# A six-stage decoder on one core: tokens quantized and the residual added by GpSimd in the feed-forward stage, tokens loaded first in three stages

## The reference, cut to what matters

```python
def _act_quant(x):
    scale = 127.0 / jnp.clip(jnp.max(jnp.abs(x), axis=-1, keepdims=True), 1e-05)
    xq = jnp.clip(jnp.round(x * scale), -128.0, 127.0) / scale
    return x + jax.lax.stop_gradient(xq - x)

def _bitlinear(x, w):
    return jnp.einsum('bsi,oi->bso', _act_quant(x), _weight_quant(w))
...
    return _bitlinear(gate * up, w_down)
```

## Time and profile before

| | |
|---|---|
| median of 3 runs | 3903.01 us (3902.52 to 3906.85) |
| profiled execution | 3898.5 us, its span 3896.7 us |
| busy over the span | PE 85%, DVE 81%, ACT 71%, POOL 67% |
| stages, from the timeline | first 0 to 333, cross-attention 337 to 842, expert 845 to 1229, Mamba 1232 to 3132, second cross-attention 3135 to 3568, feed-forward 3571 to the end |
| granted TensorE clock | 0.948 of full over the span |

### The profile page before, as it was taken

One profiled execution on the slowest core, in us unless ns is written; L12 is line 12 of the kernel. 1 busy time (PEld: TensorE's weight loads), 2 busy tenths in 40 slices (PEclk: granted clock), 3 DMA queues, 4 the chain that ended last, 5 costly groups with the idle time before them and its releaser, 6 DMA issues. The chain is left out here.

```text
span 3896.7 us, 75270 instructions
## 1 busy us (share of the span) xinstructions
PE 3307.6 (85%) x23328; PEld 2500.1 (64%) x23360; DVE 3169.0 (81%) x5291; ACT 2775.3 (71%) x5061; POOL 2609.6 (67%) x2794
## 2 busy tenths in 40 slices
PE   8996888879964688898898889888888869997887
PEld 5664666667542467676777767676766757775554
DVE  5665888855386799899899989989999759998888
ACT  2223777744475788888888888888888647777777
POOL 1222666630085699999899988989999836664555
PEclk9998999979976899999999999999999989999999
DMA  1111122242112111111111111111111112221111
GB/s 60 56 56 53 41 51 51 45 101 51 48 44 72 42 51 56 54 48 55 49 52 55 56 54 48 53 51 51 54 50 50 41 48 74 72 53 56 61 54 39
DMA packets 285487, 209.64 MB, mean 54 GB/s; under 512 B 131353, under 2 KB 249689, under 8 KB 285161
## 3 DMA queue, kind: packets, MB, share of 16 engines
q1 hardware_dynamic: 285160, 205.72, 19.0%
HBM read 149.18 MB, written 51.41 MB: 51 GB/s over the span
## 5 line engine op out<-in xcount | busy, mean ns | idle before, releaser
L2884 POOL TENSOR_TENSOR ma_ch<-ma_h,ma_crep 128x512 f32<-128x512 f32 x1024 | 1371.8, 1361 | 157.0 <-DVE ma_h L2986 142.8
L2986 DVE TENSOR_TENSOR_SCAN ma_h<-ma_a,ma_pbu 128x512 f32<-128x512 f32 x1024 | 1212.7, 1206 | 173.7 <-PE ma_pbu L2564 114.1
L2564 PE MATMUL ma_pbu<-ma_ident,ma_bu 128*128 128x128 f32 x4096 | 660.3, 285 | 198.9 <-DVE ma_h L2986 158.6
L2564 PEld LDWEIGHTS ma_pbu<-ma_ident,ma_bu 128*128 128x128 f32 x4096 | 480.3, 145 | 440.8 <-DVE ma_h L2986 312.6
L2771 ACT ACTIVATE ma_a<-ma_dt,ma_A 128x510 f32<-128x510 f32 x1024 | 653.3, 718 | 1.4 <-issue 1.4
L2573 PE MATMUL ma_py<-ma_ident,ma_ch 128*128 128x128 f32 x4096 | 626.2, 279 | 0.8 <-POOL ma_ch L2884 0.8
L2762 ACT ACTIVATE ma_bu<-ma_uT,ma_b_t 128x512 f32<-128x512 f32 x784 | 508.1, 718 | 17.1 <-PE ma_pbu L2564 15.4
L2573 PEld LDWEIGHTS ma_py<-ma_ident,ma_ch 128*128 128x128 f32 x4096 | 497.6, 145 | 1.2 <-POOL ma_ch L2884 1.2
L1571 POOL TENSOR_TENSOR xa_prob<-xa_e,xa_rec_head 128x616 f32<-128x616 f32 x128 | 155.7, 1218 | 126.0 <-DVE xa_rec_head L1663 113.9
L921 POOL TENSOR_TENSOR xa_prob<-xa_e,xa_rec_head 128x616 f32<-128x616 f32 x128 | 155.7, 1217 | 109.3 <-DVE xa_rec_head L1013 93.1
L359 POOL TENSOR_TENSOR la_veps<-la_mv,la_eps 128x2 f32<-128x2 f32 x32 | 6.3, 197 | 249.9 <-DVE la_mv L392 249.9
(11 more groups left out here) (372 smaller groups left out, 8007.0 us busy)
## 6 DMA issues: line engine op xcount, KB each, us to landing
ma_crep<-ma_ct_dram SPq DMA_DIRECT2D x256, 256.0 KB
xa_x<-act SPq DMA_DIRECT2D x64, 256.0 KB, 3.0
act<-xa_y SPq DMA_DIRECT2D x64, 256.0 KB, 3.1
la_x<-in_x SPq DMA_DIRECT2D x32, 256.0 KB, 2.6
act<-la_y SPq DMA_DIRECT2D x32, 256.0 KB, 2.2
ea_x<-act SPq DMA_DIRECT2D x32, 256.0 KB, 11.5
act<-ea_x SPq DMA_DIRECT2D x32, 256.0 KB, 4.0
ma_x<-act SPq DMA_DIRECT2D x16, 512.0 KB, 4.6
```

The source lines that it names most:

```text
L2564: last = pe.transpose(pbu[c % 2][:, t * P:(t + 1) * P], bu[:, s % 2, t, c * P:(c + 1) * P], ident[:, :])
L2884: pool.tensor_tensor(ch[:, s % 2, c], h[:, s % 2, c], crep[:, s % 4, :], ALU.mult).then_inc(multiplied, 1)
L2986: dve.tensor_tensor_scan(out=h[:, s % 2, c, :], data0=a[:, s % 2, c, :], data1=pbu[c % 2][:, :], initial=0.0, op0=ALU.mult, op1=ALU.add).t ...
```

## The change

In the feed-forward stage the quantization of the tokens (`scale_x`) goes from ScalarE to GpSimd, with a spacer before it, and waits there for the previous batch's transposes. ScalarE instead scales the down product out of PSUM into a new tile `scaled` (`scale_down`), GpSimd adds x to it (`residual`), and VectorE keeps the statistics alone (`moments`). In the first stage the identity and the tokens of batch 0 are loaded before the weights and turned before the wait for them. In both cross-attentions the token load goes out after the eighth of the 12 spreads. In the second one batch 0 is turned before the wait for the weights, and the bias work comes after its scores. In the expert stage the first group of tokens is loaded and waited for in two halves.

```diff
         block = st.block()
-        loads = ((ident[:, :], ident_d), (blocks[:, :], blocks_d),
+        loads = ((blocks[:, :], blocks_d),
                  (wq[:, :, :], wqT.rearrange("(c p) f -> p c f", p=P)),
...
         def _(sp):
+            sp.dma_start(ident[:, :], ident_d).then_inc(i_loaded, 16)
+            sp.dma_start(x[:, 0], batch_tiles(x_in, 0)).then_inc(x_loaded[0], 16)
             for dst, src in loads:
                 sp.dma_start(dst, src).then_inc(w_loaded, 16)
-            for b in range(PER):
+            for b in range(1, PER):
                 sp.dma_start(x[:, b], batch_tiles(x_in, b)).then_inc(x_loaded[b], 16)
...
+            pe.wait_ge(i_loaded, 16)
+            turn(0, 0)
             pe.wait_ge(w_loaded, 16 * len(loads))
-            turn(0, 0)
             in_turns(pe, batch, B // PER, PER, (0, 1, -1))
...
+            turned(0, 0)
             act.wait_ge(w_loaded, 16 * len(loads))
-            turned(0, 0)
             in_turns(act, batch, B // PER, PER, (0, 1, -1))
...
-            def spread_v(n):
+            def spread_v(n, meanwhile=None):
...
                     sp.wait_ge(oT_made, 2 * n - 2)
-                for lo, hi in pieces:
+                for i, (lo, hi) in enumerate(pieces):
+                    if meanwhile is not None and i == 8:
+                        sp.wait_ge(res_added, meanwhile)
+                        load_x((meanwhile + 3) % 4, meanwhile + 3)
                     h, k = lo // CTX, lo // P
...
                 if n + 1 < B:
-                    spread_v(n + 1)
-                if n >= 1 and n + 3 < B:
-                    sp.wait_ge(res_added, n)
-                    load_x((n + 3) % 4, n + 3)
+                    spread_v(n + 1, n if n >= 1 and n + 3 < B else None)
                 if n >= 3:
...
+            pe.wait_ge(setup_done, 1)
+            turn_x(0, 0, None)
+            turn_ctx(0, 0)
             pe.wait_ge(w_loaded, 16 * len(loads))
-            pe.wait_ge(setup_done, 1)
+            project_kv(0, 0)
+            project_q(0, 0, None)
+            scores(0, 0, 0)
             if bv_d is not None:
...
                 last.then_inc(bv_turned, 1)
+            turn_x(0, 1, None)
+            if bv_d is not None:
                 pe.wait_ge(bv_copied, 1)
...
                 pe.wait_ge(bo_ready, 1)
-            turn_x(0, 0, None)
-            turn_ctx(0, 0)
-            project_kv(0, 0)
-            project_q(0, 0, None)
-            scores(0, 0, 0)
-            turn_x(0, 1, None)
             batches(pe, batch)
...
                 norm_apply(0, 0)
+            copy_x(0, 0)
+            copy_ctx(0, 0)
             act.wait_ge(w_loaded, 16 * len(loads))
             if bq_d is not None:
-                act.wait_ge(bv_turned, 1)
-                act.activation(bvT[:, :, :].rearrange("p c q -> p (c q)"), pG[0][:, 0:D], ACT.Copy).then_inc(bv_copied, 1)
                 act.activation(bq4[:, :], bqk[:, 0, :], ACT.Copy, scale=0.25).then_inc(bq4_ready, 1)
                 act.wait_ge(bq4_ready, 1)
-            copy_x(0, 0)
-            copy_ctx(0, 0)
             if normed:
...
             copy_q(0, 0)
+            if bv_d is not None:
+                act.wait_ge(bv_turned, 1)
+                act.activation(bvT[:, :, :].rearrange("p c q -> p (c q)"), pG[0][:, 0:D], ACT.Copy).then_inc(bv_copied, 1)
             expo(0, 0, 0)
...
             dve.sem_inc(setup_done, 1)
-            if bv_d is not None:
-                dve.wait_ge(w_loaded, 16 * len(loads))
-                dve.wait_ge(bv_made, 1)
-                dve.tensor_tensor(bo[:, :], bo[:, :], pG[0][:, D:2 * D], ALU.add).then_inc(bo_ready, 1)
             if normed:
...
             unit(0, 0, 1)
+            if bv_d is not None:
+                dve.wait_ge(w_loaded, 16 * len(loads))
+                dve.wait_ge(bv_made, 1)
+                dve.tensor_tensor(bo[:, :], bo[:, :], pG[0][:, D:2 * D], ALU.add).then_inc(bo_ready, 1)
             sums(0, 0, 0)
...
                 for g in range(NG):
-                    for s in range(SP):
-                        sp.dma_start(x[s * B:(s + 1) * B, g * G8:(g + 1) * G8, :], xg_in[g][s]).then_inc(x_loaded[g], 16)
+                    parts = 2 if g == 0 else 1
+                    for part in range(parts):
+                        tiles = slice(part * G8 // parts, (part + 1) * G8 // parts)
+                        for s in range(SP):
+                            sp.dma_start(x[s * B:(s + 1) * B, g * G8:(g + 1) * G8, :][:, tiles, :],
+                                         xg_in[g][s][:, tiles, :]).then_inc(x_half if part < parts - 1 else x_loaded[g], 16)
                     if g == 0:
...
                 def turn(u):
-                    if u % UG == 0:
+                    if u == 0:
+                        pe.wait_ge(x_half, 16 * SP)
+                    elif u % UG == 0 or u == UG // 2:
                         pe.wait_ge(x_loaded[u // UG], 16 * SP)
...
                 pe.wait_ge(hT_copied, count(tile))
-                pe.wait_ge(res_added, count(tile))
+                pe.wait_ge(d_scaled, count(tile))
                 if is_first(tile):
...
+            def scale_down(tile):
+                k = tile[1]
+                act.wait_ge(down_made, count(tile))
+                act.wait_ge(fd_ready, count(tile))
+                act.wait_ge(r_ready, count(tile))
+                act.activation(scaled[:, k % 2], pd[:, 0:D], ACT.Copy, scale=fd[:, k % 4:k % 4 + 1]).then_inc(d_scaled, 1)
+
             def scale_h(tile):
...
-            def scale_x(tile):
-                k = tile[1]
-                m = k // 2
-                act.wait_ge(xs_ready, batch_count(tile))
-                for t in range(T):
-                    last = act.activation(xr[:, t], x[:, m % XB, t], ACT.Copy, scale=xscale[:, m % 4, t:t + 1], bias=ROUND)
-                last.then_inc(xr_ready, 1)
-
             def copy_h(tile):
...
                 k = tile[1]
-                act.wait_ge(xT_made, batch_count(tile))
+                act.wait_ge(xT_made, batch_count(tile) + 1)
                 act.activation(xT[:, k // 2 % 2], px[:, :, :, :], ACT.Copy, bias=-ROUND).then_inc(xT_copied, 1)
...
                     gate(n1)
-                if odd and n3 is not None:
-                    scale_x(n3)
+                if n_2 is not None:
+                    scale_down(n_2)
                 if n is not None:
...
             act.sem_inc(g_ready, 1)
+            act.sem_inc(d_scaled, 1)
             weight(0)
...
+            def scale_x(tile):
+                m = tile[1] // 2
+                pool.wait_ge(xs_ready, batch_count(tile))
+                pool.wait_ge(xT_made, batch_count(tile))
+                pool.tensor_tensor(x_spacer[:, :], eps[:, :], eps[:, :], ALU.add)
+                for t in range(T):
+                    last = pool.tensor_scalar(xr[:, t], x[:, m % XB, t], xscale[:, m % 4, t:t + 1], ROUND, ALU.mult, ALU.add)
+                last.then_inc(xr_ready, 1)
+
             def factor_d(tile):
...
                 pool.tensor_tensor(fd[:, k:k + 1], hunit[:, k:k + 1], wmean[:, 2:3], ALU.mult).then_inc(fd_ready, 1)
+
+            def residual(tile):
+                k = tile[1]
+                pool.wait_ge(d_scaled, count(tile) + 1)
+                pool.tensor_tensor(r[:, k % 4, :], scaled[:, k % 2], x[:, k // 2, k % 2, :], ALU.add).then_inc(r_ready, 1)
...
             def slot(odd, n_2, n_1, n, n1, n2, n3, n4):
+                if n_2 is not None:
+                    residual(n_2)
                 if n is not None:
...
                     finish(n_2)
+                if odd and n3 is not None:
+                    scale_x(n3)
                 if not odd and n4 is not None:
...
             link(pool.memset(minus_half[:, :], -0.5))
+            pool.sem_inc(r_ready, 2)
+            pool.sem_inc(xT_made, 1)
             pool.wait_ge(wmean_ready, 1)
...
-            def residual(tile):
-                j, k = tile
-                q = k % 4
-                dve.wait_ge(down_made, count(tile))
-                dve.wait_ge(fd_ready, count(tile))
-                dve.wait_ge(y_ready, count(tile))
-                link(dve.scalar_tensor_tensor(out=r[:, q, :], in0=pd[:, 0:D], scalar=fd[:, q:q + 1],
-                                              in1=x[:, k // 2, k % 2, :], op0=ALU.mult, op1=ALU.add))
-                dve.sem_inc(res_added, 1)
+            def moments(tile):
+                q = tile[1] % 4
+                dve.wait_ge(r_ready, count(tile) + 2)
                 link(dve.bn_stats(stats[:, q, :], r[:, q, :]))
...
                 if n_2 is not None:
-                    residual(n_2)
+                    moments(n_2)
                 if not odd and n4 is not None:
...
-            link = Chain(dve, chain, 6 * BT)
+            link = Chain(dve, chain, 5 * BT)
             def weight(m):
...
             dve.sem_inc(h_ready, 1)
-            dve.sem_inc(res_added, 1)
-            dve.sem_inc(y_ready, 4)
             weight(0)
...
```

24 lines of the change are left out of this document (13 added, 11 removed).

## The result

The changed kernel takes 3871.11 us (median of 4 runs, 3870.56 to 3875.34) against 3904.5 us for the kernel before on the same chip: ratio 0.9921, 95% interval 0.9909 to 0.9934, so **33 us faster** by the medians (26 to 36 by the interval). The prediction said 3931 us and slower. The two profiled spans differ by 27.3 us (3896.7 and 3869.4); the kernel before was a little faster in its profiled execution than in its median.

The account below looks back on a forecast made before the run. VectorE was taken to bound the feed-forward stage at 9.46 us a pair. Feed-forward +47.4 us, less 3.2, 8, 2.3 and 6.2 elsewhere, plus 0.5, gave +28 on 3903: 3931 us, own range 3921 to 3946, 8 in 10 down to 3880.

Parts of the forecast that it names:

- I take 1.23, since that row is GpSimd's own: Feed-forward stage: one GpSimd quantization priced at 1.23 us, from y's row of the same operation name, shape and type.
- the ring through VectorE's statistics: Feed-forward: statistics wait for GpSimd's residual, its y chain for them; 10.95 us a pair against 9.46, +44.7 us.
- rival 1: Feed-forward: GpSimd quantizes as fast as VectorE, 0.407 us, ring 9.31 us, total 3880 us; chance 0.15.
- the first cross-attention: Earlier token load removes VectorE's token waits, partly taken back by waits for exponentials: -8 us, ends +1 and -13.
- second cross-attention: Its start: tokens and context turned inside the weight wait, so the key projection starts earlier; -6.2 us.
- the halves: Expert attention: half the bytes suffice before TensorE starts, -2.3 us, ends 0 and -3.6.
- first attention: First stage: batch 0's transposes and copies fall into the weight wait, queries at 10.15 us; -3.2 us.
- the end: End of feed-forward: the last tile pays for scaling, add and hand-overs, less the removed residual; +0.6 us.
- the start of the feed-forward stage: First quantization, now on GpSimd, finishes later, so the first up projection is late: +2.1 us.
- ScalarE's edit: Feed-forward: ScalarE loses two quantizations and gains two scalings a pair, costed at nothing in the steady stretch.
- The rival "no ring": Feed-forward: only the busiest engine counts, GpSimd's 9.2 us set the pair, total 3878 us; chance 0.05.
- The clock rival: Feed-forward: TensorE idles more and drops to 1.2 GHz, its pair of about 7.3 becomes 14.7 us, 4042 us; chance 0.03.

Follow-up runs that it names:

- e2: Changed kernel with the quantization's constant read from a 128x1 tile instead of standing in the instruction; 3878.6 us, ratio 0.9932 to the kernel before.
- e9: Changed kernel with the quantization's second operation written as subtraction of minus the constant, same numbers; 3916.2 us, ratio 1.0023 to the kernel before.
- e11: Changed kernel with feed-forward y written without a subtraction, using two small GpSimd products made beforehand; 3868.8 us, ratio 0.9904 to the kernel before.
- e6: Changed kernel with the first token group of expert attention loaded in one piece again; 3879.1 us, ratio 0.9930 to the kernel before.
- e3: Changed kernel with GpSimd's quantization moved ahead of the down factor and the y chain; 3869.0 us, ratio 0.9906 to the kernel before.
- e8: Changed kernel with y's operations swapped, multiply then subtract, and one small GpSimd product added; 3885.0 us, ratio 0.9948 to the kernel before.
- e1: Kernel before with only the feed-forward part of the change; 3907.2 us, ratio 1.0006 to the kernel before.

## Why the prediction was wrong

**The step that failed** is the quantization: "I take 1.23, since that row is GpSimd's own". It measured 0.473 us. I compared y and the quantization and found one difference, an immediate for a second per-partition scalar, which is worth 0.08 us (e2). I passed over the other, the operation: y subtracts, the quantization adds, and that is 0.68 us (e9, 1.149 against 0.473; e11, 1.22 to 0.55). Of the error of 61 us (+28 forecast, -33.4 measured) this is 43: e9, which has nearly the price that I took, is 9.8 us above the kernel before, still 18 below the forecast.

**The mechanism was right.** The order on GpSimd, the ring through VectorE's statistics, and where the wait would show, all came as written; with the measured price the same sum gives 9.44 for 9.35. That was rival 1, with 9.31 for a price of 0.407, and its decision point (0.76 us) was on the right side of both prices. I gave it 0.15. That this rival's 3880 us lie near the 3871 measured is in part an accident of the other terms: the first cross-attention alone gave 9 us more than it counts. The Trainium skill (GPSIMD Engine Reference, section When to use GPSIMD) has one-input work there at roughly line rate: the row agrees for multiply and add, 0.473 us against VectorE's 0.407, and disagrees once a subtraction is in it, 1.149. I let y's rows speak against the rule as a whole, where they spoke of one operation.

**The first cross-attention** was the second error, -17.4 for -8. VectorE's work between the two marks is the same (busy 381.4 us before, 381.2 after), so the difference is in its waits: 13.0 us less for tokens, 1.5 less for its own residual, and 2.9 less for the exponentials, which I had expected to take part of the 13.0 back. Only the first two repeat. Between the marks VectorE waits 16.6 to 18.1 us for tokens in the traces without the moved load and 3.5 to 3.9 in those with it, and for the exponentials 25.9 to 30.2 without and 24.0 to 27.1 with, so the 2.9 are partly scatter between traces. The whole stretch took 453.4 to 456.6 us without the moved load and 435.6 to 439.2 with it. My own other end of the range, -13, was too small.

**The other terms** held: second cross-attention -7.4 for -6.2, the halves -2.5 or more for -2.3 (e6), first attention -1.7 (the queries start at 11.02 us, not 10.15; over all traces the mark is at 339.8 to 342.5 with the change and at 342.8 to 344.5 without) for -3.2, the moved load in the second cross-attention 0 for +0.5, and the end +1.4 for +0.6: the add and the scaling cost 0.13 us more than I had, and the last residual starts 0.7 us late, behind the y of the tile before on GpSimd (its scaling ends at 3861.20, it starts at 3861.99). At the start of the feed-forward stage I had +2.1; the first up projection came 1.3 us later, since the first quantization took 1.35 us, and by tile 4 only 0.4 was left. The sum left out one thing, the longer routing, +4.4. In the steady stretch I cost ScalarE's edit at nothing; in the first ring that is right, in the second one its scaling is a link.

The rival "no ring" fell: it had GpSimd's busy time as the bound. The clock rival fell as well: the granted clock is 1.00 in the feed-forward stage even in e9, with TensorE busy 74.5 of 100 us. Its price was also too low: TensorE's pair is 82.3% of 9.46 us, 7.8 us, and not 7.3.

## What to carry to other kernels

A price taken from a row of the same engine, operation name and shape is only good if the arithmetic operations in it are the same; write the two instructions next to each other and list every difference before choosing. Where two prices decide the sign, the chance must follow from how well the row fits, not from how many times it repeats. And when work leaves the busiest engine, walk the chain from each wait back to itself, with everything an in-order engine does in between: two such rings at 9.35 and 9.19 us held this stage while no engine was busy for more than 88 of 100 us (the changed kernel, e3, e11), and swapping two neighbours on the waiting engine gave what moving work did not.

## What was not expected of the hardware

- On GpSimd a 128x256 f32 TENSOR_SCALAR takes 0.473 us with a multiplication by a per-partition scalar and the addition of a constant, 0.554 with two per-partition scalars, and 1.149 and 1.22 in the same two forms when one operation is a subtraction, first or second (e2, e8, e9, e11). VectorE's row with a subtraction takes 0.407.
- Two of the 64 GpSimd quantizations of the changed kernel, the first of each of the first two batches, take 1.35 and 1.44 us where the others take 0.47, and the first small factor of the stage 1.07 against 0.20 later.
- The routing part of the expert stage starts at the 1.2 GHz level, after TensorE had idled between the stages (16.0 us before, 13.3 in the changed kernel), and rises to 2.4 GHz later in the changed kernel. Busy time of the engines and granted clock (third number from the end) before:

```profile
852.80:880.80 28.00, 27.98 (x138) 27.77 (x139) 7.61 (x26) 7.67 (x14) 0.00 (x0) 0.51 1.13 224
```

and in the changed kernel:

```profile
829.80:857.80 28.00, 28.00 (x135) 27.77 (x136) 7.60 (x25) 7.67 (x14) 0.00 (x0) 0.50 1.11 222
857.80:866.00 8.20, 8.20 (x43) 8.20 (x44) 3.56 (x13) 2.39 (x4) 0.00 (x0) 0.54 1.04 173
```

The work is the same, and TensorE busy throughout. By these mean clocks (level 1.2 is 0.50) the higher level comes after about 27 us in one and about 36 in the other. Eight more us at half the clock are 4 us, about the 4.4 of the table. The routing part took 93.5 and 93.6 us only in the two traces with the stage starts and loads of the kernel before (the profiled one and e1), and 97.8 to 98.8 us in all others, with halves or without, with the moved loads or without. The idle time before it doesn't decide it alone: it is 16.1 us in e6, where the rise comes after 36 us. What decides it stays open; no run changed it by itself.
